# First edge layer computed during the count matrix phase and loaded by the edge loop

## What is computed

```
hid = jax.nn.silu(edge_length_embedded @ fc_w0 / np.sqrt(NB))     # (E, 8) @ (8, 64)
w = hid @ fc_w1 / np.sqrt(RN)                                     # (E, 64) @ (64, 256)
wA, wB, wC, wD = (w[:, :MUL], w[:, MUL:2 * MUL], w[:, 2 * MUL:3 * MUL], w[:, 3 * MUL:])
xs0, xs1 = h0[edge_src], h1[edge_src]
midA = wA * xs0 * sh0        # midB, midC and midD in the same way from xs0, xs1, sh0, sh1
y0 = jax.ops.segment_sum(mid0, edge_dst, num_segments=Nn) * inv_nb
```

## Time and profile before

| what | value |
| --- | --- |
| median of three runs | 3843.97 us |
| span of the profiled execution | 3966.1 us |
| PE busy in the span | 3642.8 us, 92% |
| DVE, ACT, POOL busy | 2451.9, 1491.9, 665.9 us |
| mean granted TensorE clock | 0.968 |
| count matrix phase, from the first to the last matmul | 44.7 to about 316 us |
| edge loop | 2647 to 3354 us |

### The profile page before, as it was taken

One profiled execution on the slowest core, in us unless ns is written; L12 is line 12 of the kernel. 1 busy time (PEld: TensorE's weight loads), 2 busy tenths in 40 slices (PEclk: granted clock), 3 DMA queues, 4 the chain that ended last, 5 costly groups with the idle time before them and its releaser, 6 DMA issues. The chain is left out here.

```text
span 3966.1 us, 60201 instructions
## 1 busy us (share of the span) xinstructions
PE 3642.8 (92%) x18935; PEld 3087.8 (78%) x18935; DVE 2451.9 (62%) x4843; ACT 1491.9 (38%) x3475; POOL 665.9 (17%) x658
## 2 busy tenths in 40 slices
PE   5999899999999999999996999988888888869996
PEld 2555699999999998999994888657777777848885
DVE  7886655555555555556554666556666665677775
ACT  0363311211211111112114544457777775136663
POOL 0002000000000000000002200025555553012221
PEclk9999999999999999999997999989999999879998
DMA  1353022222222222222222210112222222431113
GB/s 53 65 105 65 26 87 89 65 89 84 70 84 74 80 88 71 83 83 71 83 69 98 72 31 30 42 47 83 81 84 79 84 80 59 150 71 38 38 38 119
DMA packets 265216, 288.48 MB, mean 73 GB/s; under 512 B 70331, under 2 KB 237327, under 8 KB 264283
## 3 DMA queue, kind: packets, MB, share of 16 engines
q1 hardware_dynamic: 233701, 208.44, 18.1%
q0 software_dynamic: 24192, 66.15, 5.8%
q10 hardware_dynamic: 7030, 10.16, 0.7%
HBM read 242.21 MB, written 42.48 MB: 72 GB/s over the span
## 5 line engine op out<-in xcount | busy, mean ns | idle before, releaser
L1043 PE MATMUL bank<-a_wide,parts 125*128 125x448 f32 x4200 | 872.9, 367 | 0.0
L1043 PEld LDWEIGHTS bank<-a_wide,parts 125*128 125x128 f32 x4200 | 785.6, 188 | 78.4 <-issue 9.9
L2288 POOL DMA_INDIRECT rows<-h_dram,src_t x392 | 375.4, 958 | 331.9 <-DVE prod L2483 218.7
L2421 ACT ACTIVATE hot<-eq,ea 128x80 f32<-128x80 f32 x1568 | 405.3, 352 | 1.0 <-DVE eq L2463 0.5
L1093 DVE CAST a_wide<-a_cols 125x2240 fp32r<-125x2240 bf16 x210 | 275.5, 1328 | 138.7 <-PE bank L1043 138.7
L1017 POOL TENSOR_TENSOR nf_g<-nf,nf_g 128x896 fp32r<-128x896 f32 x42 | 95.4, 2271 | 1575.0 <-ACT nf_g L1187 1575.0
L2328 PEld LDWEIGHTS bank<-prod,hot 128*80 128x80 f32 x2352 | 295.9, 153 | 70.9 <-issue 21.6
L2328 PE MATMUL bank<-prod,hot 128*80 128x128 f32 x2352 | 331.8, 277 | 10.6 <-issue 10.4
L1052 PE MATMUL bank<-nf_g,whh 128*128 128x448 f32 x1512 | 339.7, 369 | 0.0
L1052 PE MATMUL bank<-msg,wc 128*128 128x448 f32 x1512 | 339.1, 369 | 0.0
L1052 PEld LDWEIGHTS bank<-msg,wc 128*128 128x128 f32 x1512 | 284.2, 188 | 27.5
(11 more groups left out here) (438 smaller groups left out, 5787.7 us busy)
## 6 DMA issues: line engine op xcount, KB each, us to landing
a_cols<-a_dram SPq DMA_DIRECT2D x210, 546.9 KB
a_dram<-a_cols SPq DMA_DIRECT2D x15, 1250.0 KB, 9.9
w<-in_w SPq DMA_DIRECT2D x4, 2728.0 KB
deg_bc<-deg_dram SPq DMA_DIRECT2D x42, 224.0 KB, 6.0
gate_bc<-gate_dram SPq DMA_DIRECT2D x42, 224.0 KB, 3.2
rows<-h_dram,src_t POOLq DMA_INDIRECT x392
w<-y_rows SPq DMA_DIRECT2D x12, 512.0 KB, 15.1
w<-in_w SPq DMA_DIRECT2D x6, 896.0 KB
```

Source lines behind the costliest of these rows:

```text
L1043: ins = nc.tensor.matmul(p_msg[f][:, 0:GW], parts[0:SPB, m, c * HB + k, f * 128:(f + 1) * 128], a_wide[u % 2][0:SPB, k, :], start=(c == 0 ...
L2288: nc.gpsimd.indirect_dma_start(out=rows[n % ITC][:, :], out_offset=None, in_=h_dram, in_offset=bass.IndirectOffsetOnAxis(ap=src_t[:, n:n + ...
L2421: ins = nc.scalar.activation(hot[:, q % 2, j, m, :], eq[:, q % 2, j, :], ACT.Copy, scale=ea4[:, q * UC + j, m:m + 1])
```

## The change

The first edge layer is moved to the count matrix phase, in 49 pairs of units (NIT = 49).

- `setup` loads `edge_attr_8` ahead of `x_rows` on ACT's queue, ACT rounds it (two copies of 1568 columns), POOL subtracts (two instructions of 1568 columns), ACT's queue stores both parts, 16 rows in all. The same work leaves `gnn_to_experts`.
- `adjacency`: SP loads `fw0`, now 48x128 with a block for each unit of a pair, and the 48 rows of `ea8_dram` of a pair, three pairs ahead (three DMAs each). POOL splits `fw0`. PE makes one 128x512 matmul per pair at the end of a tile, 128 rows being 64 hidden values of two units. ACT takes the silu twice one tile later, once rounded and once not, POOL subtracts, and SP stores both parts (128x2x512 float32) to `hid_dram` two tiles later. Pair i is on tile 2 + i * 73 // 49, so tiles 2 to 73 have at most one pair each, two of three tiles have one. `hid` has two buffers, banks 4 to 7 take turns. A `max` with 0 is added to ACT's register arithmetic of each tile.
- `norm_and_galerkin` makes no `fw0` and clears no `ea8`.
- `edge_convolution`: `hidden`, `silu` and `split` are gone. SP loads the two parts of each unit, 64 rows each, to one of HIDS = 7 buffers, and `weights` reads those.

```diff
@@ setup
+                act.dma_start(ea[:, :], A["ea8"].rearrange("a (p n) -> (a p) n", p=EP)).then_inc(ea_in, 16)
                 act.dma_start(x_rows[:, :, :], A["x_rows"]).then_inc(x_in, 16)
+                act.wait_ge(ea_in, START + 16)
+                for h, cut in enumerate(ea_cuts):
+                    nc.scalar.activation(ea_parts[0][:, cut], ea[:, cut], ACT.Copy).then_inc(ea_high, 1)
...
+                for h, cut in enumerate(ea_cuts):
+                    pool.wait_ge(ea_high, START + h + 1)
+                    nc.gpsimd.tensor_tensor(ea_parts[1][:, cut], ea[:, cut], ea_parts[0][:, cut], ALU.subtract).then_inc(ea_low, 1)
@@ adjacency
+        fw = sb(ctx, "fw", [48, 128], F32R)
+        ea = [sb(ctx, f"ea{b}", [48, UE], F32R) for b in range(3)]
+        hid = sb(ctx, "hid", [128, 2, PARTS, UE], F32R)
...
+                for i in range(3):
+                    edges(i)
+                for n, (start, tiles) in enumerate(sets):
+                    for t in range(start, start + tiles):
+                        for i in pairs_of(t - 2):
+                            sp.wait_ge(hid_mm, START + i + 1)
+                            edges(i + 3)
+                            sp.wait_ge(hid_low, START + i + 1)
+                            sp.dma_start(hid_dram[i].rearrange("m p e -> p m e"), hid[:, i % 2, :, :].bitcast(F32)).then_inc(hid_out[i % 2], 16)
+                    sp.wait_ge(cols_done, START + (start + tiles) * HALVES)
+                    sp.dma_start(a_dram[:, :, start * DW:(start + tiles) * DW], a_cols[n % 2][:, :, 0:tiles * DW]).then_inc(a_stored[n % 2], 16)
...
+                for i in range(NIT):
+                    pool.wait_ge(silu_done, START + i + 1)
+                    nc.gpsimd.tensor_tensor(hid[:, i % 2, 1, :], hid[:, i % 2, 1, :].bitcast(F32), hid[:, i % 2, 0, :], ALU.subtract)\
+                      .then_inc(hid_low, 1)
...
+                    for i in pairs_of(t):
+                        pe.wait_ge(fw_step, START + 3)
+                        pe.wait_ge(ea_in[i % 3], START + i // 3 * 48 + 48)
+                        pe.wait_ge(silu_done, START + i - 3)
+                        nc.tensor.matmul(bank[4 + i % 4][:, :], fw[:, :], ea[i % 3][:, :], start=True, stop=True).then_inc(hid_mm, 1)
...
+                        for i in pairs_of(t - 1):
+                            act.wait_ge(hid_mm, START + i + 1)
+                            act.wait_ge(hid_out[i % 2], START + i // 2 * 16)
+                            for m in range(PARTS):
+                                to = hid[:, i % 2, m, :]
+                                ins = nc.scalar.activation(to if m == 0 else to.bitcast(F32), bank[4 + i % 4][:, :], ACT.Silu, scale=8.0 ** -0.5)
+                            ins.then_inc(silu_done, 1)
@@ edge_convolution
-                        sp.wait_ge(hid_mm, units + q - 1)
-                        sp.dma_start(ea8[0:24, b, :].bitcast(F32), ea8_dram[:, q * UE:(q + 1) * UE]).then_inc(ea_in[b], 16)
+                        sp.wait_ge(w_mm, chunks + max(q - HIDS + 1, 0) * UC)
+                        for m in range(PARTS):
+                            sp.dma_start(hid[m * MUL:(m + 1) * MUL, q % HIDS, :].bitcast(F32),
+                                         hid_dram[pair, m, u * MUL:(u + 1) * MUL, :]).then_inc(hid_in[q % HIDS], 16)
...
-                        if q + 2 < NU:
-                            hidden(q + 2)
...
-                        if q + 2 < NU:
-                            silu(q + 2)
...
-                            split(q + 2)
```

More of the change, by code:

```diff
@@ L295, in setup @@
         range_i = sb(ctx, "range_i", [NRANGE, 1], I32)
+        ea = sb(ctx, "ea", [128, NCH * EC // EP])
+        ea_parts = [sb(ctx, f"ea_part{m}", [128, NCH * EC // EP], F32R) for m in range(PARTS)]
         with nc.Block() as block:
@@ L827, in _, with adjacency, pairs_of @@
                         copy_back(s - 1)
[L830 to L833 removed]
+def adjacency(nc, A, sems, sb, bank, hots, a_dram, a_stored, x_rows, eps_t, stat, mean_var, std, rstd, att_w, att_in,
+              ea8_dram, hid_dram):
+    (rel_done, first_done, first_used, more_done, more_used, cols_done, stat_done, aggr_done, std_done, fw_in, fw_step,
+     ea_in_0, ea_in_1, ea_in_2, hid_mm, silu_done, hid_low, hid_out_0, hid_out_1) = sems(*("a_" + s for s in (
+        "rel first_done first_used more_done more_used cols stat aggr std fw_in fw_step "
+        "ea_in_0 ea_in_1 ea_in_2 hid_mm silu hid_low hid_out_0 hid_out_1").split()))
+    ea_in, hid_out = (ea_in_0, ea_in_1, ea_in_2), (hid_out_0, hid_out_1)
+    def pairs_of(t):
+        return [i for i in range(NIT) if FIRST_TILE + i * (NDT - 6) // NIT == t]
     hot_lo, edge_at, tile_at, iota_at, ranges = hots
@@ L934, in _ @@
                 ranges_at, turns, _, rounds = begin(act, "act")
+                more = act.alloc_register("a_more_act")
                 def relative(t):
@@ L1461, in _, with gnn_to_experts @@
                                                      scale=1.0).then_inc(z_done, 1)
-def gnn_to_experts(nc, A, sems, sb, bank, ident, eps_t, nf, x_rows, gates, raw, raw_in, ea8_dram):
+def gnn_to_experts(nc, A, sems, sb, bank, ident, eps_t, nf, x_rows, gates, raw, raw_in):
     (w_in, b2_zero, back, added, stat_done, aggr_done, std_done, rstd_done, shift_done, normed, turned, copied, hid_mm, hid_done,
-     lg_mm, step, ex_done, iota_done, top_done, ea_in, ea_high, ea_low, ea_stored) = sems(*("j_" + s for s in (
-         "w_in b2_zero back added stat aggr std rstd shift normed turned copied hid_mm hid lg_mm step exp iota top "
-         "ea_in ea_high ea_low ea_stored").split()))
+     lg_mm, step, ex_done, iota_done, top_done) = sems(*("j_" + s for s in (
+         "w_in b2_zero back added stat aggr std rstd shift normed turned copied hid_mm hid lg_mm step exp iota top").split()))
     count = E0
-    EP = 128 // 8
     groups = [(0, 2), (2, 5), (5, 10), (10, 15), (15, 20), (20, 25)]
@@ L2353, in _ @@
                     next_round(pe, regs, per_round)
-                units, chunks, dmas = at_round(pe, regs, per_round)
+                units, chunks, loads = at_round(pe, regs, per_round)
                 pe.wait_ge(added, units)
@@ L2408, in _ @@
                     units, chunks = at_round(act, regs, per_round)
-                    def silu(q):
-                        act.wait_ge(hid_mm, units + q + 1)
-                        act.wait_ge(hid_done, units + q - 1)
-                        nc.scalar.activation(hid_raw[:, q % 2, :], p_hid[:, 0:UE], ACT.Silu, scale=8.0 ** -0.5)\
-                          .then_inc(silu_done, 1)
                     def weighted_hots(q):
@@ L3103, in layouts @@
     pad8[:, :E0] = i["L0_ffn_router_w2"]
+    fw0 = np.zeros((3, 2, 8, 2, MUL), np.float32)
+    for u in range(2):
+        fw0[:, u, :, u, :] = np.asarray(i["L1_gnn_fc_w0"])
     vec = np.concatenate([np.arange(MUL)] + [MUL + 3 * np.arange(MUL) + k for k in range(3)])
```

156 lines of the change are left out of this document (72 added, 84 removed).

## The result

The changed kernel takes 3889.43 us (3887.34 to 3895.03, four runs) against 3844.27 us: ratio 1.012, 95% interval 1.0106 to 1.0135. It is slower by 45 us; 14 were forecast, in a range of 3815 to 3886. One thing must be said to read what follows: on two of the five chips that the experiments used, the kernel before takes 3967 us and not 3844, and what differs between the chips is the edge phase (the other phases agree within some 3 us); by its own edge phase, 783.1 us, the profile of before is of that kind, so its span of 3966.1 us is no outlier. The profile after (span 3886.6 us, edge phase 631.4) is of the other kind.

A forecast was written before the change was run, and what follows sets the result against it. PE was taken as the bound, with DVE close behind in the count matrix phase. Edge loop -27.6, setup +5.5, routing -0.9 and count matrix phase +37 gave +14 on 3844: 3858 us, range 3815 to 3886.

The forecast's parts named there:

- the edge loop: Edge loop: PE loses 98 x 0.22 = 21.6 us and the first product comes 6 us earlier, sum -27.6.
- The stalls of the profiled loop: Edge loop: 136 us above undisturbed units, partly stalls, taken as the profiled run's 122.1 us surplus and not credited.
- Setup: Setup: POOL's subtraction holds DVE, +6.8 us; ACT's table load moves beside DVE's work, -1.3; sum +5.5.
- nothing on DVE needs early: Setup: loading 1.6 MB of edge_attr_8 ahead of x_rows on ACT's queue costs nothing.
- Routing: Routing: the 5-column DVE instruction gets short again, -0.9 of its 1.00 us.
- Count matrix phase: Count matrix phase: 21 us for held DVE and PE plus 16 for the queue, +37, bounds 10.8 and 84.
- The held DVE, 21 us with PE's slots in it: Count matrix phase: DVE stands during 49 POOL subtractions of 1.26 us; less its idle time, with PE's 1.3, 21 us.
- PE's own work, "49 x 0.22 = 10.8 us": Count matrix phase: PE gets 49 matmuls, 10.8 us; where DVE misses time, PE's 0.22 hides in its wait.
- The queue, 16 us: Count matrix phase: pair loads 4.3 us late behind eight set stores, 34 us, half beside counted shortfalls: +16, bounds 0 and +43.
- The third rival: Count matrix phase: the queue stalls in full, ten sets at 4.3 us, 43 instead of 16: 3885 us, chance 0.15.
- its sign: Count matrix phase: ACT waiting for the pair's store at most sets would show the third rival.
- The first and second rivals: First: count matrix marks not held, 3825 us, chance 0.18. Second: edge loop gives 32 us more, 3826 us, chance 0.12.

The follow-up runs named there:

- e10: The change with hidden values stored once, unsplit, from four buffers, six load buffers, setup's subtraction on DVE, DVE splitting in the loop: 3852.83 us, ratio 1.0020.
- e5: The change without POOL's 49 subtractions in the count matrix phase: 4032.68 us, ratio 1.0160, on a chip where the kernel before takes 3967 us.
- e16: e10 with only the first four of its 49 pair stores: 3836.14 us, ratio 0.9984.
- e6: The change with only the first two of the 49 pair stores: ratio 1.0089.
- e7: The change with only the first two of the 49 pairs in the count matrix phase: 3964.42 us against 3967.0, ratio 0.9991.

## Why the prediction was wrong

**What bounds the kernel, and the edge loop**: right. -27.6 was forecast; the difference of times gives -28.7 (some 27 without what lies behind the loop), the unit 5.58 us for 5.60, the first product 5.4 us after the first load's issue instead of 10.3, so -4.9 for -6. DVE and ACT lost their work in the loop for nothing, as said. The stalls of the profiled loop were rightly left out of the sum, but for a wrong reason: they were not one execution's, they belong to some chips, and there the change's loop saves next to nothing. That the timed runs fell on the other kind of chip is luck.

**Setup**: +9.0 for +5.5. The hold was sized well (6.5 for 6.8), though the comparisons, which were to show it, kept their length and two other instructions were held. ACT's table load did move out of the phase, where the first marks now come 1.7 us after its first instruction and not 3.1. The step that failed is "nothing on DVE needs early": with 1.6 MB ahead of `x_rows` the small transfers of the chunk ends came late, and DVE waited 2.13 us; with `x_rows` behind ACT's roundings (e8) they came in time. The two do not add up but overlap: without the hold DVE would have waited some 8.6 us (an estimate, 2.13 + 6.5), as it did in e10 (8.58), and with the ends in time setup became only 1.8 us shorter.

**Routing**: the 5-column instruction is back to 0.15 us from 1.00, as forecast; the phases between the count matrix and the loop gave 4.0 us in all, 3.4 of them in the routing phase itself (61.0 us instead of 64.4) where 0.9 was forecast. What gave the other 2.5 was not traced.

**Count matrix phase**: +68.9 for +37, and this is the miss. Its parts fell otherwise than the sum had them.

- *The held DVE, 21 us with PE's slots in it.* The hold is there: the marks went from 476 to 567 ns (x344), both forms together are busy 39.8 us more, and the earlier trace rows was a fair guide to it, 0.8 us per subtraction instead of 1.26. But e5 takes the subtraction away and gains 3.4 us. DVE had idle time again because PE was standing for something else.
- *PE's own work, "49 x 0.22 = 10.8 us".* It is 17.5 (e16), since a pair's matmul takes PE 0.36 us here. And 12.8 us more (280.25 - 267.44) go to the lower clock, by an estimate from these two traces; the sum put it at nothing: the marks' matmuls of one form take 417 ns in the change, 393 in e16 and 392 before, with the same work.
- *The queue, 16 us.* This is the step that failed: "behind a set's store of 9.8 us they are 4.3 us late", eight times, "and half of it runs beside shortfalls already counted". The stops are nine, 5.3 us each on average, and nothing halves them: it was DVE's shortfall that hid in PE's stops, and not the stops in the shortfall. 48.1 us stand where 16 did, and my upper bound of 43 was too low too. The count was off as well: by the earlier trace rows and the sum's own rule (a DMA share above 0.4) eleven sets fall in those windows, 3, 4 and 4, and not eight.
- *The third rival* (3885, a chance of 0.15) had the stops in full and nearly the price, and its sign came: ACT waits 51.5 us for pair stores, 11 times. That its price came so near is luck in part, for it holds 21 us for DVE, which e5 prices at 3.4, and nothing for the clock. And what spoke for it in the text, the DMA share and the price per byte, is not what stops PE: e6 has hardly any of these bytes and 39.1 of the 48.1 us. From 287.0 to 383.5 us the sets' stores are 19.3 us apart in the change, and the same ones 18.6 in e6; before it was 10.3. What could have been read from the rows is the landing of a set's store beside that period, 9.8 of 10.3 us: a load that is issued behind it comes some 10 us later, and the text itself gave such a load 5.5 us.

The first and second rivals fell: marks are held, and the loop gave no more than forecast.

By the rule of the Trainium skill ("SBUF — State Buffer", "SBUF: two separate sides") the subtraction and a mark, which reads one tensor, exclude each other for a whole instruction if the mark runs in a two-port mode. The marks' longest, 1559 ns where 472 is the median and a subtraction takes 1352, agree with an exclusion; that the marks run in such a mode is not shown here. The rows sized the hold; whether a hold is paid for was the question.

## What to carry over

Ask of every transfer that is added to a phase what it will stand behind in its queue, as landing time of the regular store against the time between two of them, before asking about the engines: there were 10.3 us for a store of 9.8. Count the ring of buffers on each side of the added work against that store's landing; lengthening one ring alone only moved the wait to the next (48 us on PE, then 62 on ACT, then 18 on `a_cols`). Terms that stall the same engine must not be added and halved by feel: here the longest one was paid, and the hold went into it but for 3.4 us. And a stop costs more than its length: the clock was 0.92 over the phase, and some 13 us of PE's time went with it (an estimate, the 12.8 above).

## What the hardware showed that I had not expected

- The hold goes the other way too. POOL's first subtraction in setup took 12.79 us beside DVE's row of 64 comparisons, which kept their 11.18 us exactly; the second, beside single DVE instructions, took 3.80. The two instructions of DVE that were held, 3.46 and 3.73 us, stand behind the row of comparisons. Those 64 short instructions without a gap were not delayed at all, and POOL's was.
- Issuing three small loads behind a set's store took SP 5.3 to 6.2 us, 14 times, instead of some 1.9 (0.6 each, in the median), and what stands behind in its list waits too. With the sets' stores on the other queue (e1) it took 3.8 at most. By what SP is held the trace does not show.
- The edge phase of the changed kernels took 630 to 633 us on three chips and 774 to 780 on two others, with the same gathers (946 ns each on POOL in the change, 961 in e7). On the second kind ACT waits some 4 us for PE's sums again and again, in e7 mostly every 9 or 19 us. The cause stays open.
